# A feed-forward stage of a software-pipelined Trainium2 kernel: two engines' order within a turn, a third buffer, and later weight loads

## The reference, cut to what matters

```
h = layernorm(x, ln1_g, ln1_b)
h = bitlinear(h, w1, b1)          # 256 -> 1024
h = gelu(h, approximate=False)
h = layernorm(h, ln2_g, ln2_b)
h = bitlinear(h, w2, b2)          # 1024 -> 256
```

## Time and profile before

| what | us |
|---|---|
| median of 3 runs | 420.19 |
| lowest and highest of them | 415.25, 420.78 |
| the profiled execution's own time | 417.46 |
| its span | 415.7 |
| busy in the span: PE, DVE, ACT, POOL | 335.3, 305.9, 264.2, 181.8 |

### The profile page before, as it was taken

The page is one execution under the profiler, slowest core; times in us unless marked ns, Lnnn a source line. Parts: engine busy times, 40 slices in busy tenths (PEclk is TensorE's granted clock), DMA queues, the critical chain, the costliest instruction groups (busy, mean ns, idle before and its releaser), DMA issues.

```text
span 415.7 us, 9146 instructions
## 1 busy us (share of the span) xinstructions
PE 335.3 (81%) x3086; PEld 237.1 (57%) x3093; DVE 305.9 (74%) x1025; ACT 264.2 (64%) x567; POOL 181.8 (44%) x207
## 2 busy tenths in 40 slices
PE   2999589889999999832877777778488999999864
PEld 2777467667677776610554455446265666666421
DVE  2798645778998988577899999985436777787741
ACT  1565435654545545734798898886668888888520
POOL 1214400211211355128999899982005555445520
PEclk9999989999999999955789999999689999999985
DMA  8399999995463450000000000000001222212000
GB/s 238 124 273 288 322 232 320 251 183 110 84 140 86 113 67 3 1 0 0 2 1 2 0 2 2 2 0 2 0 13 29 39 53 53 52 41 39 26 25 25
DMA packets 43725, 33.68 MB, mean 81 GB/s; under 512 B 19872, under 2 KB 39712, under 8 KB 43552
## 3 DMA queue, kind: packets, MB, share of 16 engines
q1 hardware_dynamic: 43680, 33.11, 32.3%
HBM read 24.71 MB, written 8.39 MB: 80 GB/s over the span
## 4 chain that ended last, share of the span: by engine, by line
PE 49%; DVE 19%; issue 14%; ACT 6%; DMA 4%; POOL 4%; SPq 3%; DVEq 0%; POOLq 0%; ACTq 0%
PE PS L1458 5%; DVE sm L738 4%; PE PS L1235 4%; PE PS L1448 4%; DMA kst<-scr_k 4%; PE PS L1224 4%; PE PS L1214 3%; PE PS L1215 3%; PE PS L1293 3%; PE PS L1254 3%; PE PS L1154 3%; PE PS L1443 3%; PE PS L1421 3%; SPq L315 2%; DVE sm L710 2%
## 5 line engine op out<-in xcount | busy, mean ns | idle before, releaser
L988 ACT ACTIVATE pT<-PS 128x512 f32<-128x512 f32 x64 | 36.6, 596 | 52.5 <-PE PS L1215 52.4
L603 DVE TENSOR_REDUCE negm<-PS 128x4 bf16<-128x512 f32 x64 | 42.3, 684 | 16.5 <-PE PS L1224 16.3
L432 POOL TENSOR_TENSOR sm<-sm,mhalf 128x1 f32<-128x1 f32 x16 | 11.3, 709 | 87.5 <-DVE sm L635 87.5
L448 POOL TENSOR_TENSOR kst<-kst,rows 128x1024 f32<-128x1024 f32 x16 | 37.7, 2356 | 6.4 <-ACT kst L1056 6.2
L1100 ACT ACTIVATE lnT<-PS,Atok 128x128 f32<-128x128 f32 x128 | 36.4, 369 | 3.6 <-PE PS L1399 2.0
L1215 PE MATMUL PS<-identb,negm 128*128 128x128 bf16 x256 | 35.7, 223 | 0.0
L1333 PE MATMUL PS<-identf,w2f 128*128 128x128 f32 x128 | 19.0, 297 | 20.2 <-ACT w2f L1045 20.2
L462 POOL TENSOR_TENSOR kst<-kst,rows 128x1024 f32<-128x1024 f32 x14 | 33.1, 2364 | 0.0
L1235 PE MATMUL PS<-pT,vx 128*32 128x128 f32 x512 | 27.3, 287 | 5.0 <-ACT pT L988 5.0
L1333 PEld LDWEIGHTS PS<-identf,w2f 128*128 128x128 f32 x128 | 15.1, 150 | 24.5 <-ACT w2f L1045 19.2
L1458 PE MATMUL PS<-wd,xT 128*128 128x392 f32 x64 | 27.2, 552 | 1.8 <-DVE rest L882 1.8
(11 more groups left out here) (220 smaller groups left out, 976.2 us busy)
## 6 DMA issues: line engine op xcount, KB each, us to landing
scr_q<-qpart SPq DMA_DIRECT2D x8, 384.0 KB, 4.0
scr_k<-kpart SPq DMA_DIRECT2D x8, 384.0 KB, 5.1
rows<-in_rows SPq DMA_DIRECT2D x1, 2056.0 KB, 9.4
X<-in_x SPq DMA_DIRECT2D x8, 256.0 KB, 4.9
CTXT<-in_ctxT SPq DMA_DIRECT2D x8, 256.0 KB, 4.5
vx<-in_ctx SPq DMA_DIRECT2D x16, 128.0 KB, 3.1
out<-rest SPq DMA_DIRECT2D x16, 128.0 KB, 1.7
qst<-scr_q SPq DMA_DIRECT2D x8, 192.0 KB, 4.7
```

The source lines that it names most:

```text
L448: gp.tensor_tensor(n2[q.slot], n2[q.slot], ln2g, ALU.mult).then_inc(b_g2, 1)
L603: v.tensor_reduce(negm[f.slot % 2][:, 4 * hg:4 * hg + 4], PS[:, 2 + hg % 2, :].rearrange("p (h k) -> p h k", h=4), AX_X, ALU.max, negate=T ...
L988: s.activation(pT[:, hg, :], PS[:, hg % 2, :], ACT.Exp, scale=float(DH0) ** -0.5).then_inc(a_e, 1)
```

## The change

- DVE's turn of the feed-forward runs `hidden(b)` ahead of `scale2(c)`.
- ACT's turn runs norm of `p`, gelu of `b`, levels of `c`, in this order and ahead of the store of `f`; before it was levels, store, gelu, norm.
- `n2` gets a third buffer, and the norm waits for the levels of the block three before (`done(act, b_u2, p, -2)`) instead of two.
- The rows (gains and biases) are loaded in two parts; the second part, w1, w2 and the small weights are issued at blocks 8, 5, 6 and 9 instead of 2 to 5; weight sums, means and roundings come two turns later. POOL's `scale_rows` also waits for the second part of the rows.
- PE's and POOL's orders in `turn_b` stay as they are.

```diff
-        n2 = 2 * [kst[i].rearrange("p h t -> p (h t)").bitcast(F32) for i in range(2)]
+        n2 = [kst[i].rearrange("p h t -> p (h t)").bitcast(F32) for i in range(2)] + [sb("n2_2", [128, F])[:]]
 ...
                 if part == 0:
-                    sp.dma_start(rows[:], A["rows"].partition_broadcast(128)).then_inc(s_rows, 16)
+                    sp.dma_start(rows[:, 0:4 * D], A["rows"][0:4 * D].partition_broadcast(128)).then_inc(s_rows, 16)
 ...
+                elif part == 3:
+                    sp.dma_start(rows[:, 4 * D:], A["rows"][4 * D:].partition_broadcast(128)).then_inc(s_rows2, 16)
 ...
-                if f and isinstance(f.b, int) and 2 <= f.b < 6:
-                    load_weights(f.b - 2)
+                if f and f.b in (2, 5, 6, 8, 9):
+                    load_weights((2, 5, 6, 8, 9).index(f.b))
 ...
+                pool.wait_ge(s_rows2, 16)
                 pool.wait_ge(s_wq, 3)
 ...
-                    if c.b == 3:
+                    if c.b == 5:
                         weight_means()
 ...
-                if c and 4 <= c.b < 10:
-                    ternary_step(c.b - 4)
-                if c and c.b == 10:
+                if c and 6 <= c.b < 12:
+                    ternary_step(c.b - 6)
+                if c and c.b == 12:
                     sum_weights()
 ...
             def turn_b(tau, _a, b, _p, q, c, d, _e, _f, _g):
+                if b:
+                    hidden(b)
                 if c and c.b < NB - 1:
                     scale2(c)
 ...
-                if b:
-                    hidden(b)
                 if d:
 ...
-                    if isinstance(f.b, int) and f.b in (3, 4):
-                        weight_sum(f.b - 3)
+                    if f.b in (5, 6):
+                        weight_sum(f.b - 5)
 ...
+                if p:
+                    act.wait_ge(b_sh, tau - 1)
+
+                    done(act, b_u2, p, -2)
+                    s.activation(n2[p.b % 3], gl[p.slot], ACT.Identity, scale=rs23[tau % 2][:, 0:1],
+                                 bias=sh23[tau % 2][:, 0:1]).then_inc(b_n2, 1)
+                if b:
+                    gelu(b)
                 if c:
 ...
-                    s.activation(u2, n2[c.slot], ACT.Copy, scale=sm3[c.slot][:, 3:4], bias=MAGIC).then_inc(b_u2, 1)
+                    s.activation(u2, n2[c.b % 3], ACT.Copy, scale=sm3[c.slot][:, 3:4], bias=MAGIC).then_inc(b_u2, 1)
 ...
-                if b:
-                    gelu(b)
-                if p:
-                    act.wait_ge(b_sh, tau - 1)
-
-                    done(act, b_u2, p, -1)
-                    s.activation(n2[p.slot], gl[p.slot], ACT.Identity, scale=rs23[tau % 2][:, 0:1],
-                                 bias=sh23[tau % 2][:, 0:1]).then_inc(b_n2, 1)
 ...
-                    if isinstance(c.b, int) and c.b == 3:
+                    if c.b == 5:
```

More of the change, by code:

```diff
@@ L158, in build @@
         s_const = sem("constants_ready"); s_cc = sem("constants_chain")
-        s_wq = sem("weight_means_chain"); s_tq = sem("ternary_chain"); s_sr = sem("rows_scaled"); s_rows = sem("rows_loaded")
+        s_wq = sem("weight_means_chain"); s_tq = sem("ternary_chain"); s_sr = sem("rows_scaled"); s_rows = sem("first_rows_loaded"); s_rows2 = sem("other_rows_loaded")
         s_wsum = sem("weight_sums_ready"); s_wtot = sem("weight_totals_ready")
@@ L447, in turn_b @@
                     pool.wait_ge(b_n2, q.b + 1)
-                    gp.tensor_tensor(n2[q.slot], n2[q.slot], ln2g, ALU.mult).then_inc(b_g2, 1)
+                    gp.tensor_tensor(n2[q.b % 3], n2[q.b % 3], ln2g, ALU.mult).then_inc(b_g2, 1)
                 if p or e:
@@ L461, in turn_b @@
                     pool.wait_ge(b_g2, q.b + 1)
-                    gp.tensor_tensor(n2[q.slot], n2[q.slot], ln2b, ALU.add).then_inc(b_h2, 1)
+                    gp.tensor_tensor(n2[q.b % 3], n2[q.b % 3], ln2b, ALU.add).then_inc(b_h2, 1)
             turn_a(*peeled(NB, NB, 4, 4))
@@ L731, in biased @@
                 dve.wait_ge(b_h2, q.b)
-                v.tensor_tensor(n2[q.slot], n2[q.slot], ln2b, ALU.add).then_inc(b_h2, 1)
+                v.tensor_tensor(n2[q.b % 3], n2[q.b % 3], ln2b, ALU.add).then_inc(b_h2, 1)
             def scale2(c):
@@ L737, in scale2 @@
                 dve.wait_ge(b_h2, c.b + 1)
-                top = q3.mark(v.tensor_reduce(zc[:, 0:1], n2[c.slot], AX_X, ALU.max, apply_absolute_value=True))
+                top = q3.mark(v.tensor_reduce(zc[:, 0:1], n2[c.b % 3], AX_X, ALU.max, apply_absolute_value=True))
                 dve.wait_ge(b_c3, top)
```

## The result

| | before | after |
|---|---|---|
| median, us | 420.49 | 447.74 |
| lowest and highest, us | 415.25, 421.21 | 445.81, 450.72 |
| span of the profiled execution, us | 415.7 | 445.0 |

The changed kernel is slower: the ratio is 1.0685, with a 95% interval of 1.0633 to 1.0737. The forecast was 439, in a range of 427 to 450. `hidden` is L700 in the changed kernel, the levels L1056, their transposes L1336, `up` L1205, the norm L1046, gelu L1026; some of them move by a few lines in the kernels of the experiments.

The account below looks back on a forecast made before the run. DVE, ACT and POOL were taken as almost equally full, a loop of `scale2`, levels, gelu and `stats2` closing at 6.07 us. 11.3 + 4 + 3.7 + 5 - 1.7 - 1.5 = +20.8 on 417.46 gave 438.3, stated as 439; range 427 to 450.

Parts of the forecast that it names:

- The loop through `up`, `hidden` and `scale2`: Feed-forward turn: levels to end of `up` 4.40 us, release 0.04, `hidden` 1.20, `scale2` 1.69; 7.33 us a turn.
- the second through the column transposes, norm and gelu: Feed-forward turn: levels to end of PE's `columns` 4.61 us, then ACT's copy, gate bias, norm, gelu; also 7.33 us.
- The term +11.3: Nine feed-forward steps from turn 7 on, each taking 7.33 instead of 6.07 us: +11.3 us.
- The three steps ahead of turn 7: Feed-forward steps still without gate products, half clock for one and a half of them: +4 us, bounds +0.5 and +6.
- The first turns: Turn 3: gelu of block 2 waits behind block 1's norm, delaying the first levels: +3.7 us, bounds +2 and +5.
- The mis-sized term: Feed-forward: PE's longer idle time makes its clock fall in three of nine turns, 1.7 us each: +5 us.
- The rival "in every turn": Feed-forward: PE's clock falls in all nine turns, +15 us instead of +5, total 449 us; chance 0.16.
- PE's gap of about 2.7: PE idle about 2.7 us in one piece each new feed-forward turn; the longest gap before was 1.18 us.
- The end: Last feed-forward turns, levels of block 12 to those of block 15: 14.06 to 12.4 us, -1.7, bounds 0 and -3.4.
- The loads: Attention turns: later weight loads spare the scores of blocks 4 and 5 stack waits: -1.5 us, bounds 0 and -2.5.
- POOL's new wait: POOL's wait for a load issued four turns before the instruction behind it: costs nothing.
- The faster rival: Feed-forward: `hidden` first lets gelu start earlier, the turn falls to 5.84 us, total 411.5 us; chance 0.06.

Follow-up runs that it names:

- the second run of the loads alone: Repeat of the kernel before with only the later weight loads, both engines' orders and the two buffers kept: 418.22 us, ratio 0.9975.

## Why the prediction was right, and where its size was off

The direction, the mechanism and most terms came out; the time, 447.7, lies 9 above the point and inside the range. The forecast sum was +20.8 us and the two spans differ by 29.3; one term holds nearly all of the difference.

- The loop through `up`, `hidden` and `scale2`, and the second through the column transposes, norm and gelu, 7.33 us each: measured 7.34 at full clock. That each alone holds the turn was shown by the two runs with one order back, and that they go through PE's order by the two that move its steps on PE. The term +11.3 measured +11.4.
- The three steps ahead of turn 7: +4, measured +3.7.
- The first turns: +3.7, measured +3.7, but the step behind it, that gelu's place in turn 3 is the cause, was too short. POOL releases the norm late in turns 3 and 4 (and after that, once ACT has caught up), and everything behind the norm waits.
- **The mis-sized term is the clock.** The prediction took three falls at 1.7 us, +5. The granted clock fell in seven of nine turns, and lost 14.3 us, from 1.3 to 2.8 us a turn, as the run with the filled gap shows. Two things were wrong in it. The number of falls was chosen between none and all because a full burst of work lies between the gaps; it did not protect. And the price was taken from one fall of 3.4 us at half clock. It fits the four steps of 8.66 to 8.92 us, whose mean granted clock was 0.80 or 0.81 and which lost 1.3 to 1.6 us each. In the three of 9.96, 10.16 and 10.18 us it was 0.66, and they lost 2.6 to 2.8 us: there the clock stayed at about 0.5 for 6 us and more, and transposes, gate products and `up` all ran at 1.2 GHz. That the low clock lasted because the slowed work itself lasts longer fits this, but no run shows it, and no run shows why two of the nine turns with the same gap had no fall. The rival "in every turn", 449 at 0.16, was the nearest, partly by luck: it had too many falls, nine, at too low a price, 1.7.
- PE's gap of about 2.7: measured 2.83 in most turns (2.67 to 2.93).
- The end: -1.7 was for the levels of block 12 to those of block 15, and -1.0 was measured there; another 0.5 came behind them, which the sum did not have, so the -1.5 in all agrees by luck. The clock took part here too: it was 0.70 over the step behind block 12's levels. With both loops open and the clock at 1.00 the same stretch took 11.81 us, 2.2 less than before. The loads: -1.5, measured -1.5. POOL's new wait and the steps moved by two turns cost nothing that the attention turns show (7.50 all the same, but for the one of 8.46 with the weight means).
- The faster rival, 411.5, asked for `up` ahead of the transposes. With PE's order changed in that way, both loops open, the turn was 5.95 and not 5.84, and the whole no faster than before: the loop of levels, transposes, copy, norm and gelu is as long as the turn, DVE has no gap left either, and the first turns cost what the turns and the end gain. PE did not run `up` ahead of what stands before it in its list: DVE waited 1.52 us for it in the turn shown.

## What to carry to other kernels

Before you move an instruction forward in one engine's list, follow its input back to the engine that makes it and see what that engine does ahead of it; if that waits, a turn earlier, for something now behind the moved instruction, the two have closed a loop whose length is the new turn. Here the product was ready 1.55 us early, and the loop through it was still 1.26 us longer than the old turn (7.33 against 6.07), since `hidden` (1.20) and `scale2` (1.69) now follow each other behind it. And an idle gap on PE is only free while PE is off the path. Once it is on it, price the work behind the gap at half clock, and in most turns rather than in some: here it was seven of nine.

## What the runs showed of the hardware that was not expected

A gap of 2.83 us in each turn, with 4.5 us of solid work between two of them, had the granted clock fall in seven of nine turns; a gap of 1.97 us did so in one of nine, and gaps of 1.2 us (before) and of 1.2 to 1.6 us (both loops open) in none of the nine. The length of the gap is not all there is to it: the kernel before had a fall in the first turns, where PE has less to do in a turn, and the second run of the loads alone had one in the last turns, 0.79 from 275.5 to 282.75, with gaps of 1.18 us. Filling the 2.83 us with 16 matmuls that nobody needs made the kernel 15.7 us faster (447.7 to 432.0), by the medians of two chips; the two spans, 445.0 and 429.3, are as far apart. The Trainium skill ("TensorE: Matmul & The Clock Gate", section "What's actually happening") has it that activity is what releases the throttle; the trace with the filled gap agrees, 1.00 against 0.83 over the same 48 us.
